# Six weight blocks of expert 0 loaded and split into parts inside the first phase

## The reference, cut to what matters

```
h = layernorm(x) * (1 + ca) + sa
x = x + ga * linear_attention(h, W_qkv, W_out)      # 16 heads of 16, rope, elu + 1
h = layernorm(x) * (1 + cb) + sb
x = x + gb * moe(h, router_w, wg, wu, wd)           # 8 experts, top 2, capacity 640
```

## Time and profile before

| | |
|---|---|
| median of 3 runs | 622.04 us (619.25 to 622.12) |
| the profiled execution's own time | 624.11 us |
| its span, first to last instruction | 622.4 us |
| steps -3 to 54 of the pipeline | up to about 206 us |
| search and placing of tokens | to about 256 us |
| experts | from 255.86 us on |

### The profile page before, as it was taken

How to read it: one execution, slowest core, us unless ns; L and a number is a source line. 1 busy time by engine, 2 the same in 40 slices (tenths; PEclk the granted TensorE clock), 3 DMA queues, 4 the chain that set the end, 5 groups by cost and what they waited for, 6 DMA issues and landing times.

```text
span 622.4 us, 13153 instructions
## 1 busy us (share of the span) xinstructions
PE 583.3 (94%) x4013; PEld 526.4 (85%) x4013; DVE 452.6 (73%) x1357; ACT 320.8 (52%) x718; POOL 269.1 (43%) x406
## 2 busy tenths in 40 slices
PE   6999999999999878899999999999999999999993
PEld 5587789898787333699999999999999999999993
DVE  4688899998899888786767667766676776566441
ACT  4688888886444333344445445445444454354331
POOL 5788857776688301302080170260350440612322
PEclk9999999999999899999999999999999999999997
DMA  6322468644666640517267067175273373450312
GB/s 174 103 68 78 116 190 247 213 145 131 198 198 188 209 121 0 151 39 218 72 119 198 23 122 206 35 139 156 62 152 116 87 144 103 103 127 8 35 19 25
DMA packets 92481, 75.29 MB, mean 121 GB/s; under 512 B 12156, under 2 KB 89094, under 8 KB 92424
## 3 DMA queue, kind: packets, MB, share of 16 engines
q1 hardware_dynamic: 82344, 57.39, 30.8%
q0 software_dynamic: 8992, 15.90, 13.7%
q10 hardware_dynamic: 1088, 1.31, 0.6%
HBM read 52.41 MB, written 22.16 MB: 120 GB/s over the span
## 4 chain that ended last, share of the span: by engine, by line
PE 59%; issue 9%; DVE 8%; DMA 3%; POOL 3%; ACT 2%; SPq 2%; POOLq 0%; ACTq 0%; DVEq 0%
PE bank L1684 28%; PE bank L1696 13%; PE bank L1717 4%; PE bank L1557 3%; DVE hit L1097 2%; PE bank L1732 2%; PE bank L1432 2%; DMA x_in<-x 1%; POOL xg L556 1%; PE bank L1635 1%; DMA q_in<-q_store 1%; PE bank L1543 1%; SPq L377 1%; PE bank L1616 1%; PE bank L1469 1%
## 5 line engine op out<-in xcount | busy, mean ns | idle before, releaser
L556 POOL DMA_INDIRECT xg<-h_rows,g_idx x40 | 43.2, 1081 | 235.6 <-DVE g_idx L1223 225.8
L1684 PE MATMUL bank<-xT_h,w_h 128*128 128x320 f32 x432 | 134.8, 312 | 1.2 <-DVE hid L1309 0.8
L1684 PE MATMUL bank<-xT_l,w_h 128*128 128x320 f32 x432 | 133.1, 308 | 0.0
L1684 PE MATMUL bank<-xT_h,w_l 128*128 128x320 f32 x432 | 132.9, 308 | 0.0
L755 ACT CAST hid_h<-hid 128x320 fp32r<-128x320 f32 x108 | 49.7, 460 | 85.9 <-DVE hid L1309 80.5
L566 POOL DMA_INDIRECT out<-yo,s_idx x40 | 66.6, 1666 | 62.1 <-DVE yo L1371 26.6
L752 ACT ACTIVATE act_g<-bank 128x320 f32<-128x320 f32 x108 | 47.2, 437 | 70.4 <-PE bank L1684 61.6
L1684 PEld LDWEIGHTS bank<-xT_h,w_h 128*128 128x128 f32 x432 | 81.1, 188 | 2.1 <-DVE hid L1309 1.0
L1684 PEld LDWEIGHTS bank<-xT_l,w_h 128*128 128x128 f32 x432 | 81.1, 188 | 0.0
L1684 PEld LDWEIGHTS bank<-xT_h,w_l 128*128 128x128 f32 x432 | 81.0, 188 | 0.0
L1696 PE MATMUL bank<-w_h,hid_h 128*128 128x256 f32 x280 | 80.2, 286 | 0.9 <-issue 0.5
(11 more groups left out here) (235 smaller groups left out, 1364.5 us busy)
## 6 DMA issues: line engine op xcount, KB each, us to landing
w_raw<-wg SPq DMA_DIRECT2D x32, 256.0 KB, 3.3
w_raw<-wu SPq DMA_DIRECT2D x32, 256.0 KB, 4.8
w_raw<-wd SPq DMA_DIRECT2D x16, 512.0 KB, 6.0
x_in<-x SPq DMA_DIRECT2D x32, 128.0 KB, 2.2
q_store<-qT SPq DMA_DIRECT2D x32, 128.0 KB, 2.2
q_in<-q_store SPq DMA_DIRECT2D x32, 128.0 KB, 2.3
x_re<-x SPq DMA_DIRECT2D x32, 128.0 KB, 2.2
out<-x SPq DMA_DIRECT2D x32, 128.0 KB, 2.2
```

Source lines behind the costliest of these rows:

```text
L556: nc.gpsimd.indirect_dma_start(out=xg[par][:, a, :], out_offset=None, in_=h2_rows, in_offset=bass.IndirectOffsetOnAxis(ap=g_idx[par][:, a: ...
L1684: last = MM(bank[2 * h + m][:, 0:HCAP], W[i][:, f, at:at + P], XT[j][:, k, cols], start=n == 0, stop=n == 3 * KC - 1)
```

## The change

The ten transfers of expert 0's weights move from steps 19 to 23 to steps 2 to 11, one in each step: first the five of blocks 0 to 3, then the five of blocks 4 to 7. Blocks 0 to 5 are split in half blocks of 384 columns, one in a step: the high part by ScalarE at the end of steps 8 to 19, the low part by VectorE in steps 9 to 20, between `ve` and `feat`. A new semaphore `half_h` counts the first half of each block, `sp_h` and `sp_l` are raised by the second. The splits of blocks 0 to 5 at their old places are removed.

```diff
+EARLY, FIRST_SPLIT = 6, 8
...
-                if 0 <= s.rep - (LAG + 1) < WEIGHT_LOADS:
-                    part = s.rep - (LAG + 1)
-                    load_weights(0, 0, raw_a, parts=(part,))
-                    load_weights(0, FC // 2, raw_b, parts=(part,))
+                if 2 <= s.rep < 2 + 2 * WEIGHT_LOADS:
+                    part = (s.rep - 2) % WEIGHT_LOADS
+                    if s.rep < 2 + WEIGHT_LOADS:
+                        load_weights(0, 0, raw_a, parts=(part,))
+                    else:
+                        load_weights(0, FC // 2, raw_b, parts=(part,))
...
+            def early_high(i):
+
+                f, cols = i // 2, slice(i % 2 * WU // 2, (i % 2 + 1) * WU // 2)
+                act.wait_ge(raw_a if f < FC // 2 else raw_b, WEIGHT_LOADS * 16)
+                nc.scalar.copy(w_h[:, f, cols], w_raw[:, f, cols]).then_inc(sp_h if i % 2 else half_h, 1)
...
+                if 0 <= s.rep - FIRST_SPLIT < 2 * EARLY:
+                    early_high(s.rep - FIRST_SPLIT)
...
-            for f in range(FC - 2):
-                split_high(0, f, f)
...
+            def early_low(i):
+
+                f, cols = i // 2, slice(i % 2 * WU // 2, (i % 2 + 1) * WU // 2)
+                dve.wait_ge(sp_h if i % 2 else half_h, f + 1)
+                ins = V.tensor_tensor(w_l[:, f, cols], w_raw[:, f, cols], w_h[:, f, cols].bitcast(F32), ALU.subtract)
+                if i % 2:
+                    ins.then_inc(sp_l, 1)
...
+                if 0 <= s.rep - FIRST_SPLIT - 1 < 2 * EARLY:
+                    early_low(s.rep - FIRST_SPLIT - 1)
...
-            for f in range(4):
-                split_low(0, f, f)
...
-            split_low(0, 4, 4)
...
-            split_low(0, 5, 5)
```

More of the change, by code:

```diff
@@ L343, in build_program @@
         raw_a, raw_b, sp_h, sp_l = (sem(n) for n in ("raw_a", "raw_b", "sp_h", "sp_l"))
+        half_h = sem("half_h")
         ga_d = [sem(f"ga_d{g}") for g in range(XG)]
```

## The result

The changed kernel takes 630.37 us (median of 6 runs, 629.03 to 632.26); the kernel before took 622.08 beside it (619.25 to 623.85). The ratio is 1.0138, 95% interval [1.0118, 1.0157]: 8.3 us slower, 7.3 to 9.8 by the interval. The profiled execution took 631.65 us around a span of 629.6. In the changed kernel the line of `early_low` is L909, `feat` L1023, `rot` L546, `rs` L509, `early_high` L618, the gather L560.

The account below looks back on a forecast made before the run. It took a ring through all engines, none idle much, to set the pace of the steps; 11.0 (VectorE) - 0.8 (loads) - 1.2 (opening) = +9.0 us on 622.04 gave 631.0 us, range 627 to 635 (chance 0.70).

Parts of the forecast that it names:

- VectorE's half blocks: Steps 9 to 20: each half block waits until 0.11 us before `rot` ends; 12.3 us, less 1.3 absorbed, 11.0 us slower.
- rival 1: Steps 9 to 20: the half blocks do not meet `rot` and VectorE slips in; 621.9 us, chance 0.12.
- The lower bound of 1.9 us: VectorE's cost in steps 9 to 20 if the half blocks did not meet `rot`: 1.9 us.
- It has room: Steps 8 to 19: ScalarE's twelve half copies of about 0.42 us fit its idle time and cost nothing.
- With the cover gone, 5.0 us: ScalarE's half copies, steps 8 to 19, would cost 12 x 0.42 = 5.0 us if not covered.
- The loads: Transfers moved to steps 2 to 11: VectorE's wait for `x_in` at 116.53 goes, -0.8 us; nothing charged at the new place.
- The opening: Opening of the experts: without the splits two gather issues shorten to 0.95 us, -1.2 us; bounds 0 and 5.8.
- The sum: Whole kernel: 11.0 - 0.8 - 1.2 = +9.0 us, giving a median of 631.0 us, 1.4% slower.
- Rival 2: Opening of the experts: the splits were the path, all six come off, 5.8 us; 617.3 us, chance 0.06.
- Rival 3: First phase: GpSimd's `rs` also pays, 0.3 us in each of twelve steps, 3.6 us more; 634.6 us, chance 0.12.

Follow-up runs that it names:

- x1: The change, with the VectorE half blocks' second input in PSUM instead of SBUF and placed behind the wait for the exponential; ratio 1.0026 to the kernel before.
- x2: The change, with the VectorE half blocks a few instructions earlier, in front of `rot_a`, when `rot` is not running; ratio 1.0025 to the kernel before.
- x4: The change's early loads and early ScalarE half copies, with all VectorE low parts at their old places; ratio 1.0034 to the kernel before.
- x13: The whole change, with the ScalarE half copies moved in front of the copy of v; ratio 1.0144 to the kernel before.
- x6: The kernel before, with the four low splits of blocks 0 to 3 left out at the opening; ratio 1.0007 to the kernel before.
- x5: The kernel before, with only the ten weight loads moved to steps 2 to 11; ratio 0.9990 to the kernel before.
- x10: The kernel before, with only VectorE's low parts at the opening reordered into its waits, loads at their old place; ratio 1.0001 to the kernel before.
- x3: Early loads and ScalarE halves, low parts at old places, plus an 8-column two-SBUF-input subtraction where the change has its VectorE half blocks; ratio 1.0119 to the kernel before.
- x11: Only loads and ScalarE halves early, the half copies in front of the copy of v, low parts at old places; ratio 1.0014 to the kernel before.
- x9: The kernel before, with early loads and VectorE's low parts at the opening spread over its waits, nothing split early; ratio 0.9981 to the kernel before.
- x12: The change with four blocks early instead of six, ScalarE halves before the copy of v, VectorE halves before `rot_a`; ratio 1.0020 to the kernel before.

## Why the prediction came out

**VectorE's half blocks: right, mechanism and size.** Predicted 1.0 us late in each of steps 9 to 13: measured 0.98 to 1.02. Steps 14 and 15: 0.28 and 0.58; the first is 0.62 less the absorbed wait for `x_in` at 66.52. Step 16: 1.25 for 1.48. Step 17: 0.09, which is 0.87 less the 0.70 of TensorE at 77.77. Step 18: 0.84 for 0.87. Steps 19 and 20: 1.28 and 1.52 for 1.48. Step 21: -0.24 for the -0.27 of 95.71. Together 10.6 for 11.0; `feat` of step 20 at 103.58, forecast 103.4. That the half block stands until 0.11 us before `rot` is through, read from one meeting over 0.73 us, held over 1.29 us. The 1.46 us of the half blocks refute rival 1, by which they would not meet, and x1 and x2 show that the meeting is the cost. The lower bound of 1.9 us was added up wrongly, though: it has nothing for step 16, which the same text lists with 19 and 20 as having no wait, so it should be about 2.4. The Trainium skill (SBUF — State Buffer, "Who interferes with whom") says besides that a VectorE instruction with at most one SBUF input, outside the modes that use both of its ports, does not contend with GpSimd. x1 agrees, with 0.56 us inside `rot`.

**ScalarE: the price was wrong, the sum was not.** "It has room" was read from 1.54 us idle in 10. That idle time was waits inside the ring at other places than the copy's, and alone the copies cost 2.5 us (x4). The second half of the sentence, that longer steps give room, is what saved it: in the change they are covered (x13). That they are covered is read from the wait that is left. "With the cover gone, 5.0 us" was too much.

**The loads: -0.8 had no ground.** The wait is absent in x6 with the old loads as well. It happened to be in the profiled execution of before, and the difference of the two profiles shows the -0.9; the runs of x5 show -0.6 us, with [-1.9, +0.6] around it.

**The opening: -1.2 was -0.7.** Both issues did fall to 0.96 and 0.95, so these issues of an indirect gather were held up by the splits; x10 shows the same with one block. The Trainium skill (SBUF — State Buffer, "Who interferes with whom") infers that a `tensor_tensor` does not hold up the making of descriptors, by which the gain would be 0; that does not hold here. But the third tile's rows follow the start of their issue. TensorE takes them 3.78 us behind it in both profiles (250.63 and 254.41 before; 261.68 and 265.46 after). That issue starts 5.01 us behind `g_idx` before and 4.29 after: the 0.7 us that the issue in front of it had been stretched by. The 0.47 us inside the third tile's own issue delayed nothing.

**The sum.** By the places that the prediction names, the traces give 10.6 - 0.9 - 0.7 = 9.0, as forecast; the runs give 8.3, and 9.0 for x13. That the 9.0 came out to the tenth is luck: 0.4 us too much in the first phase and 0.5 too much of a gain at the opening cancel, and the loads' term was an accident of one profile. Without it the traces give 9.9, just above the interval of 7.3 to 9.8. The prediction had nothing for the rest of the way: 0.8 us more between step 32 and the search, 1.0 more in the search, 3.9 less in the experts' loop. If the other runs of the change have the short loop too, their median is lower for it; the runs show only whole times, so this stays open.

**The rivals.** Rival 2, the opening as the path: x6 takes four of the six low splits away for nothing measurable, 1.0007 where 3.8 us would be 0.994. Rival 3: GpSimd's `rs` did take 0.86 us instead of 0.54 in these steps, the 0.3 us foreseen, but the steps lost 10.6 us and not 14.6, so it did not reach them. GpSimd had the time: it waits 0.86 us for `rot_b` in front of `rot` in step 10 of the change.

## What to carry to other kernels

Before an instruction is put into an idle gap of its engine, see what the neighbour engine runs in that gap: a two-input subtraction in SBUF beside GpSimd costs what is left of GpSimd's instruction, however small it is, and the cure is to move it by a few instructions or to give it an input in PSUM. Idle time in a ring of engines (each waits once a step for the one before it) is only free at the place where the wait stands, and one wait can be filled once. A gain at one place has to be followed to the next wait: the 0.7 us at the opening were gone some 20 us later in three of the kernels. A short wait seen in one execution is not a term of a sum until a second profile shows it.

## What the runs showed of the hardware

- The blocking goes both ways and is nearly exact: the one that comes second goes on 0.11 to 0.14 us before the recorded end of the first. The half block of step 9 ends at 53.04; with 0.54 us of its own (x2) it ran from 52.50, and `rot` ended at 52.62. `rs` in step 9: the half block ends 0.46 us behind its start, and it takes 0.86 instead of 0.54, so 0.32 more.
- A subtraction of 8 columns took 1.06 us (x3) beside `rot`.
- A GpSimd issue of an indirect gather is held up by a VectorE subtraction of two SBUF inputs as well: 1.41 us against 0.95 (x10). The transfer of its rows was not later for it: 3.78 us from the start of the issue to TensorE's use, with an issue of 1.42 and of 0.95 us.
- Nine of the 14 profiles have a stretch at a granted clock of 0.5 in the middle, at another place in nearly each. It is 3.4 us long (206.4 before, 221.8 in the change; two in x3, at 216.1 and 260.5, and two in x11) or 6.8 us (x9, x10); there is none in x1, x4, x5, x12 and x13. Where it fell into the search of the change, that part was 1.0 us longer. In x11 it began between 182 and 184 us, and TensorE had been busy for 0.17 us of the 2 us before; in before it was 1.37 of 2 us. Why it comes in one execution and not in another stays open.
- The experts' loop takes different times with the same code. Without ScalarE's wait of 5.1 us (the change, x1, x12) TensorE was 2.0 us faster at that place than in before. Over the four experts ahead of it the distance to before shrank by 1.9 us in the change and 2.0 in x12, by 0.8 in x1, and not at all in x10 and x13.
